# A fused attention and FFN kernel: the order of VectorE's and GpSimd's work in the first batch, the place of one weight, and the order of two slots at a batch's end

## The reference

```
xn  = layernorm(x)                                   # eps 1e-5
# attention: token mix, three projections, a decayed sum over time
xm  = xn * time_mix + shift(xn) * (1 - time_mix)     # shift by one token
k   = exp(min(xm @ Wk.T, 60)); v = xm @ Wv.T; r = xm @ Wr.T
wkv, sum_k = decayed causal sums of k*v and of k     # per head, over the 1024 tokens
att = (sigmoid(r) * wkv / (sum_k + 1e-16)) @ Wo.T
# ffn: a second layer norm, ternary weights, one clip for the whole tensor
xf  = layernorm(xn; eps 1e-3) * gamma + beta
g   = max(abs(xf)); b = mean(abs(W))
ffn = clip(xf * 128 / g, -128, 128) @ clip(round(W / b), -1, 1) * (g * b / 128)
out = x + att + ffn
```

## Time and profile before

| | |
|---|---|
| median of 3 runs | 891.2 us (890.45 to 891.48) |
| the profiled execution | 890.95 us, span 889.1 us |
| PE busy | 858.8 us (97%) |
| DVE busy | 763.8 us (86%) |
| ACT busy | 561.5 us (63%) |
| POOL busy | 185.7 us (21%) |
| phase A, batches 0 to 3 | about 16 to 422 us |

### The profile page before, as it was taken

How to read it: one execution, slowest core, us unless ns; L and a number is a source line. 1 busy time by engine, 2 the same in 40 slices (tenths; PEclk the granted TensorE clock), 3 DMA queues, 4 the chain that set the end, 5 groups by cost and what they waited for, 6 DMA issues and landing times.

```text
span 889.1 us, 12691 instructions
## 1 busy us (share of the span) xinstructions
PE 858.8 (97%) x3892; PEld 704.2 (79%) x3892; DVE 763.8 (86%) x1251; ACT 561.5 (63%) x982; POOL 185.7 (21%) x229
## 2 busy tenths in 40 slices
PE   4799999999999999999999999999999999999998
PEld 3577887688877888788888888888888888888886
DVE  6998979899898989899897897878978888789684
ACT  5596878787796888787564554545545536365441
POOL 2532415060322415070030110200201103011000
PEclk9999999999999999999999999999999999999999
DMA  9332515243433416054543245324451443424211
GB/s 320 118 130 101 185 49 180 70 155 117 155 130 115 169 50 233 12 177 135 208 147 115 83 154 189 129 71 142 153 177 57 156 142 98 151 94 143 94 48 48
DMA packets 64076, 115.61 MB, mean 130 GB/s; under 512 B 7840, under 2 KB 7840, under 8 KB 64032
## 3 DMA queue, kind: packets, MB, share of 16 engines
q1 hardware_dynamic: 64032, 115.12, 37.7%
HBM read 73.15 MB, written 41.96 MB: 129 GB/s over the span
## 4 chain that ended last, share of the span: by engine, by line
PE 71%; DVE 13%; ACT 7%; issue 6%; DMA 1%; POOL 1%; ACTq 0%; DVEq 0%; SPq 0%; POOLq 0%
PE kvr L584 14%; PE kvr L582 14%; PE kvr L583 14%; PE out_banks L623 7%; PE out_banks L625 7%; PE out_banks L602 5%; PE out_banks L605 5%; PE out_banks L604 5%; DVE scans L1085 2%; DVE absmax L993 1%; DVE bn_stats L942 1%; DVE k_and_kv L1092 1%; ACT xm_hi L748 1%; DVE k_and_kv L1075 1%; ACT gate L832 1%
## 5 line engine op out<-in xcount | busy, mean ns | idle before, releaser
L1377 POOL TENSOR_TENSOR evacuated<-normed,mix_over_ffn_row 128x512 f32<-128x512 f32 x28 | 51.2, 1829 | 336.8 <-DVE ffn_lo L1010 336.8
L582 PE MATMUL kvr<-xm_hi,wk_hi 128*128 128x512 f32 x256 | 102.8, 402 | 5.5 <-DVE xm_lo L1010 4.9
L582 PE MATMUL kvr<-xm_hi,wv_hi 128*128 128x512 f32 x256 | 102.7, 401 | 5.0 <-DVE k_and_kv L1075 4.9
L602 PE MATMUL out_banks<-wo_hi,rwkv_hi 128*128 128x512 f32 x256 | 100.1, 391 | 2.5 <-DVE rwkv_lo L1105 2.5
L582 PE MATMUL kvr<-xm_hi,wr_hi 128*128 128x512 f32 x256 | 102.0, 398 | 0.0
L584 PE MATMUL kvr<-xm_hi,wv_lo 128*128 128x512 f32 x256 | 100.8, 394 | 0.0
L583 PE MATMUL kvr<-xm_lo,wv_hi 128*128 128x512 f32 x256 | 100.3, 392 | 0.0
L584 PE MATMUL kvr<-xm_hi,wr_lo 128*128 128x512 f32 x256 | 100.0, 391 | 0.0
L584 PE MATMUL kvr<-xm_hi,wk_lo 128*128 128x512 f32 x256 | 99.9, 390 | 0.0
L583 PE MATMUL kvr<-xm_lo,wk_hi 128*128 128x512 f32 x256 | 99.8, 390 | 0.0
L583 PE MATMUL kvr<-xm_lo,wr_hi 128*128 128x512 f32 x256 | 99.7, 389 | 0.0
(11 more groups left out here) (151 smaller groups left out, 1950.1 us busy)
## 6 DMA issues: line engine op xcount, KB each, us to landing
other<-ffn_input SPq DMA_DIRECT2D x64, 256.0 KB, 5.2
x<-in_x SPq DMA_DIRECT2D x15, 1024.0 KB, 5.4
other<-in_x SPq DMA_DIRECT2D x8, 1024.0 KB, 8.7
own_ahead<-in_x SPq DMA_DIRECT2D x8, 1024.0 KB, 5.8
ffn_input<-evacuated SPq DMA_DIRECT2D x32, 256.0 KB, 4.0
ffn_input<-parked SPq DMA_DIRECT2D x32, 256.0 KB, 2.8
attn_scratch<-x SPq DMA_DIRECT2D x8, 1024.0 KB, 4.4
parked<-attn_scratch SPq DMA_DIRECT2D x8, 1024.0 KB, 6.3
```

What stands on the lines that cost most here:

```text
L582: nc.tensor.matmul(KVR[:, m, :], hi, XH[t][:, ch, :], start=(ch == 0), stop=False)
L602: nc.tensor.matmul(OUT[:, q, :], hi, WH["o"][:, j, :], start=(j == 0 and ph == "A"), stop=False)
L1377: G.tensor_tensor(U[:, n % RING, :], XN[:, ch, :], BC[:, :], ALU.mult).then_inc(pool_v, 1)
```

## The change

Six edits:

1. On DVE, batch 0 is written out ahead of the loop (`is_first=True`); the loop runs over batches 1 and 2.
2. Of the four `first_ffn_input` steps, two (channels 2 and 3) and the statistics of `other` move from ahead of batch 0 into it, to the top of group 2, behind `recurrence` of chunk 0. `weight_lo("o")` moves into groups 7 to 10, one chunk each.
3. On POOL, the four casts that make `wo_hi` move from ahead of the statistics chain of `other` to behind it; they are then ahead of the own second tile's chain (`batch_a`).
4. The raw `wo` is loaded into `x1` (`X[1]`, the place of the second tile of the batch) in place of `parked`; the load of that tile for the residual moves back in SP's queue, behind the last of the weight's four low parts.
5. ACT's evacuations of `other` slots wait for `wk_lo` alone (`CH`), no longer for all of `wo_lo` (`4 * CH`).
6. At the end of each batch of phase A, DVE takes slot 22 (`mix_or_clip`) ahead of `rwkv` of the last chunk, and slot 23 ahead of `rwkv_lo` of the last chunk; ACT takes `high_part` of slot 22 ahead of `rwkv_hi` of the last chunk.

```diff
@@ -345,7 +345,7 @@
 
 
         RAW = {"k": ZB[:, :, :], "v": X[1][:, :, :], "r": KV[:, :, :, :].rearrange("p a b n -> p (a b) n"),
-               "o": ZB[:, :, :]}
+               "o": X[1][:, :, :]}
 
         block = ctx.enter_context(nc.Block())
 
@@ -364,10 +364,8 @@
                 load_weight(n)
             sp.dma_start(ZA[:, :, :], x_t[HALF, 0]).then_inc(s_oth, 16)
             sp.dma_start(XQ[:, :, :], x_t[0, 1]).then_inc(s_own, 16)
-            sp.wait_ge(dve_w, CH)
+            sp.wait_ge(dve_w, 2 * CH)
             load_weight("o")
-            sp.wait_ge(dve_w, 2 * CH)
-            sp.dma_start(X[1][:, :, :], x_t[0, 1]).then_inc(s_x[1], 16)
 
             def store_ffn_input(b, n):
                 kind, ch = SLOTS[n]
@@ -404,6 +402,9 @@
                 sp.dma_start(ZA[:, :, :], x_t[b + HALF, 1]).then_inc(s_oth, 16)
                 store_ffn_input(b, 7)
                 store_row(b, 0)
+                if b == 0:
+                    sp.wait_ge(dve_w, 4 * CH)
+                    sp.dma_start(X[1][:, :, :], x_t[0, 1]).then_inc(s_x[1], 16)
                 store_ffn_input(b, 12)
 
                 sp.wait_ge(dve_out, BANKS + bank_use(b, "A", "attn0") + Q)
@@ -704,7 +705,7 @@
                 elif ph == "A":
                     if "other" in kind:
 
-                        act.wait_ge(dve_w, 4 * CH)
+                        act.wait_ge(dve_w, CH)
                         act.wait_ge(s_plain[ch], 16 * (2 * b + int(kind[-1])))
                         nc.scalar.activation(PLAIN[:, ch, :], bank, ACT.Copy)
                     nc.scalar.activation(U[:, r, :], Y[:, ch, :] if virtual else bank, ACT.Identity,
@@ -893,10 +894,11 @@
                 elif last is not None:
                     high_part(b, ph, last)
                 quotient(b, CHUNKS - 1)
+                if ph == "A":
+                    high_part(b, ph, len(SLOTS) - 2)
                 rwkv_hi(b, ph, CHUNKS - 1)
                 if ph == "A":
-                    for n in (len(SLOTS) - 2, len(SLOTS) - 1):
-                        high_part(b, ph, n)
+                    high_part(b, ph, len(SLOTS) - 1)
                     if not last_a:
                         other_sums(b + 1, 0)
                 if last_a:
@@ -1042,8 +1044,7 @@
             first_ffn_input(0)
             weight_lo("r")
             V.tensor_copy(last_x[:, :], FIRST[:, :, TILE])
-            for ch in range(1, CH):
-                first_ffn_input(ch)
+            first_ffn_input(1)
 
             def ternary_sum():
                 dve.wait_ge(s_w[4], 16)
@@ -1139,11 +1140,19 @@
             ADDS_AT = {5: [("other0", [0])], 6: [("other0", [1])], 7: [("other0", [2, 3])],
                        17: [("other1", [0])], 18: [("other1", [1])], 19: [("other1", [2, 3])]}
 
-            def batch(b, ph, is_last=False, last_a=False):
+            def batch(b, ph, is_last=False, last_a=False, is_first=False):
                 last = None
                 for g in range(GROUPS):
                     c, m = divmod(g, 3)
                     n = slot_ahead(g, is_last)
+                    if is_first and g == 2:
+
+                        first_ffn_input(2)
+                        first_ffn_input(3)
+                        dve.wait_ge(s_oth, 16)
+                        stats_of(1, 1, ZA, 1, "A")
+                    if is_first and 7 <= g < 7 + CH:
+                        weight_lo("o", [g - 7])
                     if ph == "A" and g == GROUPS - 2:
 
                         recurrence(b, c)
@@ -1196,11 +1205,11 @@
                 if ph == "A":
                     denominator(b, CHUNKS - 1)
                     rwkv_lo(b, CHUNKS - 2)
+                    mix_or_clip(b, ph, last + 1)
                     rwkv(b, CHUNKS - 1)
                     low_part(b, ph, last)
+                    mix_or_clip(b, ph, last + 2)
                     rwkv_lo(b, CHUNKS - 1)
-                    for n in (last + 1, last + 2):
-                        mix_or_clip(b, ph, n)
                     for n in (last + 1, last + 2):
                         low_part(b, ph, n)
                 else:
@@ -1242,10 +1251,8 @@
                 V.tensor_scalar(gamb[:, :], gam[:, :], sc[:, 2:3], None, ALU.mult)
                 V.tensor_scalar(betb[:, :], bet[:, :], sc[:, 2:3], None, ALU.mult).then_inc(dve_s, 1)
                 dve.wait_ge(dve_s, 5)
-            dve.wait_ge(s_oth, 16)
-            stats_of(1, 1, ZA, 1, "A")
-            weight_lo("o")
-            with dve.Fori(0, HALF - 1) as b:
+            batch(0, "A", is_first=True)
+            with dve.Fori(1, HALF - 1) as b:
                 batch(b, "A")
             batch(HALF - 1, "A", last_a=True)
             with dve.Fori(HALF, B - 1) as b:
@@ -1308,12 +1315,6 @@
 
             pool.sem_inc(pool_xn, 1)
             ffn_scale(0, 0, own[:, 0], 0, 0)
-
-            pool.wait_ge(dve_w, 3 * CH)
-            pool.wait_ge(s_w[3], 16)
-            for ch in range(CH):
-                G.tensor_copy(WH["o"][:, ch, :], RAW["o"][:, ch, :]).then_inc(hi_w["o"], 1)
-
             def call(b, tile):
 
                 return stats_number(b, "A", tile), stats_place("A", tile)
@@ -1382,6 +1383,9 @@
                         mix_input(b, n)
 
             other(0, "other0", first=True)
+            pool.wait_ge(s_w[3], 16)
+            for ch in range(CH):
+                G.tensor_copy(WH["o"][:, ch, :], RAW["o"][:, ch, :]).then_inc(hi_w["o"], 1)
             with pool.Fori(0, HALF - 1) as b:
                 batch_a(b)
             batch_a(HALF - 1, is_last=True)
```

## The result

| | median us | lowest to highest | runs |
|---|---|---|---|
| before | 891.08 | 890.38 to 891.66 | 17 |
| changed | 892.58 | 892.07 to 893.64 | 17 |

The ratio is 1.0019, with a 95% interval of 1.0012 to 1.0026: slower by 1.5 us. The forecast was 893.7 and +2.55; so its sign and its range (889.8 to 897.5) hold, and the size is 1.1 us too large.

A forecast was written before the change was run, and what follows sets the result against it. PE is busy 97%, but DVE was taken to bound half of batch 0. Start +5.4 and ends -2.85 give +2.55 on the profiled 890.95, 893.5; the median, 0.25 above, is 893.7; range 889.8 to 897.5.

The forecast's parts named there:

- The wait of 4.92 us: PE's wait in group 4 of batch 0 for DVE's k*v; closing it was said to bring nothing by itself.
- The start: Beginning of batch 0 up to PE's group 12: DVE's idle time was to make it +5.4 us later.
- The chain from the statistics to ACT's normalisation: For `other` in batch 0: 3.4 us taken, between a least of some 2.9 and the measured 3.85.
- DVE idle 4.1 ahead of maximum 3: In batch 0's start: DVE ready at 41.0, waiting 4.1 us for ACT's evacuation 3, which ends at 45.1.
- The clock: PE behind its long wait in batch 0: granted clock at half speed again, 1.6 us lost, now behind slot 4.
- POOL hidden behind DVE: Batch 0, slot 8: with the casts later, `normed` at 55.5 against 55.0 wanted, hidden behind DVE's +5.4.
- Rival 3: POOL decides at slot 8 as DVE and POOL disturb each other: +8.5 us, result 896.8; chance 0.12.
- The ends: Ends of batches: ACT's statistics of `other` 1.0 us earlier, 0.95 gained for each of batches 1 to 3, -2.85.
- The price of the ends: At a batch's end PE needs the last `rwkv_lo` at 122.15; it comes at 122.0, 0.1 us to spare.

The follow-up runs named there:

- Kernel 3: The changed kernel with the four inputs and the statistics of `other` back ahead of batch 0; 888.36 us, ratio 0.9969 to before.
- kernel 2: The changed kernel with edit 6 undone, so the start only; 895.56 us, ratio 1.0048 to before.
- kernel 4: The changed kernel with POOL's four casts of `wo_hi` back ahead of the chain of `other`; 893.99 us, ratio 1.0030 to before.
- kernel 6: Kernel 3 with `wo_lo` made by GpSimd behind the own second tile's chain, no longer by VectorE; 889.63 us, ratio 0.9983 to before.
- kernel 1: The kernel before with edit 6 alone, the ends of batches; 888.84 us, ratio 0.9975 to before.
- Kernel 10: Kernel 3 with ACT's quotient of chunk 2 behind slot 11's evacuation and `rwkv_hi`, `rwkv`, `rwkv_lo` of chunk 2 moved later; 889.08 us, ratio 0.9980 to before.
- kernel 7: The changed kernel with 64 transposes that nobody reads in PE's wait for `other` at slot 4; 891.96 us, ratio 1.0010 to before.

## Why the prediction was right, and where it was off

- **The wait of 4.92 us brings nothing by itself.** Right. It is gone, 9.04 us stand at slot 4 (about 10 was said), and PE's group 12 is 4.4 us later. Kernel 3, with the wait half there, is 4.2 us faster.
- **The start: +5.4 was said; +4.3 it is** (81.26 against 76.95; kernel 2 by itself 4.3). This is the term that carries the error. Up to the second k*v 3.2 was said and 2.1 came (47.49 against 45.39); the four parts of `wo_lo` and the rest make 2.2, as said (2.4 + 0.4 - 0.6). The difference lies in two steps: 0.6 ahead of the chain (DVE is done with the statistics of `other` at 36.9, where 37.5 was said; the recurrence took 4.2 us, from 28.58 to 32.82, for 4.5, and the statistics 2.9 for 3.2), and 0.6 in the chain itself; the hand-overs behind it took 0.1 more than said.
- **The chain from the statistics to ACT's normalisation: 3.4 was said, 2.8 it is** (36.92, where DVE's next instruction starts, to 39.71; the 3.85 was taken in the same way), which is about the 2.9 that I had as the least. I put it between the bounds because other DVE work would lie beside it. That work is a maximum and `bn_stats`, which read one input, and the chain ran at its least beside them; in the kernel before, at 3.85, it was `wo_lo`, a subtraction of two inputs, and four of POOL's five operations were longer there, by 1.05 us together. The rule of the Trainium skill (SBUF — State Buffer, Who interferes with whom) says that a DVE instruction with two inputs in SBUF contends with a GpSimd one that reads SBUF, and a reduction does not. The trace agrees, and kernels 4 and 6 show the other half of it. By that rule the forecast would have been 893.2, nearer to what was measured.
- **DVE idle 4.1 ahead of maximum 3:** it is 3.41, maximum 3 at 43.90 in place of 45.1, and nearly all of the difference is the step above.
- **The clock: 1.6 us lost behind the long wait.** Right in size: slot 4 to slot 5 takes 4.96 us at half speed and took 3.20 before, so 1.8 was lost. Most of the stretch at half speed, 35.8 to 45.6, lies inside the wait. At group 12 the loss counts for at most 0.6 us, because DVE is last there. In kernel 4, where PE was last, a stretch that was 2.3 us longer cost 1.0.
- **POOL hidden behind DVE: right.** The casts start at 43.71 (behind 45 was said) and `normed` is done at 53.34, where 55.5 was said, and PE has no wait for it. It was close: slot 8 starts at 53.89 (55.0 was said), so POOL had 0.5 us to spare. Rival 3 fell.
- **The ends: -2.85 was said, -2.7 it is** (+4.31 at the first wait for `rwkv_lo`, +1.63 at the last; kernel 1 by itself 2.4). The mechanism, ACT's statistics 1.0 us closer, is right and so is batch 1's and 2's share, 1.07 and 0.99. Batch 3 gave 0.62. What was wrong is where PE would give it back: the waits for `xm_lo` stayed at 1.5 us (1.53, now 1.49). What went are smaller waits ahead of them. Of the 1.07 us, 0.79 is there at slot 8 already, which before waited 0.44 us for ACT's `normed` (first row below, of before; 149.39 - 76.95 = 72.44) and now does not (second row, of after; 152.91 - 81.26 = 71.65). Kernel 10 shows why: in the middle of batches 1 and 2 ACT has no gap, the last `xm_lo` is the end of a chain of ACT and DVE behind PE's own slot 11, and its wait moves with that chain's length. Why batch 3 gave less was not tried; in its first half PE waits for nothing that the change brings closer (its wait for `xm_lo` was 0.41).

```profile
149.39 0.63 PE L526 MATMUL transposed<-ident,normed 128*128 128x128 f32 x4 [0.44 <-ACT normed L773]
```

```profile
152.91 0.60 PE L527 MATMUL transposed<-ident,normed 128*128 128x128 f32 x4
```

- **The price of the ends** (PE needs the last `rwkv_lo` at 122.15, 0.1 to spare) was not paid: PE has no wait there in the changed kernel.

+2.55, less 1.1 at the start, plus 0.15 at the ends, is +1.6, the difference of the spans; the medians differ by 1.5.

## What to carry to other kernels

A wait of the busiest engine that stands upstream of a place where the same supplier is late again can be worth nothing (the 4.92 us here): take the time of the second place, and ask how much idle time an order puts into that supplier. Latency that lies under other work (here 7 us of DVE's work over POOL's chain) is free until the work is moved away. When work is put off, look up every waiter for it, the ones that wait for the whole as well, before its new place is chosen. A low granted clock inside a wait cost nothing here (6.2 us of it): read the clock's price from how long the same instructions take behind the wait, and then from whether anybody was waiting for them.

## What the hardware showed unexpectedly

- Casts and subtractions on POOL lengthen DVE's operations beside them: two scans took 1.43 and 1.56 us instead of 1.22 and 1.20 beside casts, 1.71 and 2.25 beside two-input subtractions; a product with two inputs (`gate`) took 1.09 beside a cast and 0.69 at the batch's end. POOL loses as well: four casts took 3.22 us there, 2.30 in the kernel before.
- How long PE works at half speed behind a wait does not follow the wait's length here: 3.4 us behind 4.92 (before), 3.5 behind 9.04 (changed kernel), 5.8 behind 9.64 (kernel 4), and 3.4 behind the 2.06 of kernel 7, where the clock was full all through the wait and fell only 1.4 us behind it.
- PE's first matmul starts at 10.72 to 12.07 us in kernels whose work up to there is the same; what moves it was not looked for. Positions in the start are therefore compared from there where the kernels differ in it.
